# A quantised layer's head two tiles ahead, its tail reordered, and routing steps spread over shared chunks

## The reference

```python
x = x + _L0_xattn_ref(_layernorm(x, axis=-1), itok_BxS_13_99985, ctx_2048, ctx_2048, ctx_2048)
x = x + _L0_ffn_ref(_layernorm(x, axis=-1), L0_ffn_norm_w, L0_ffn_w_gv, L0_ffn_w_out)
x = x + _L1_xattn_ref(_layernorm(x, axis=-1), ctx_2048, L1_xattn_Wq, L1_xattn_Wg, L1_xattn_bg, L1_xattn_Wkv, L1_xattn_Wo)
x = x + _L1_ffn_ref(_layernorm(x, axis=-1), L1_ffn_gate_w, L1_ffn_w_gate, ..., L1_ffn_sw_down)
```

## Time and profile before

| | |
|---|---|
| median of 3 runs | 1104.53 us (1104.44 to 1106.37) |
| profiled execution | 1107.26 us |
| its span in the trace | 1105.5 us |
| busy: PE, DVE, ACT, POOL | 1048.1, 673.4, 591.9, 281.9 us |
| mean granted clock of PE | 0.986 |
| quantised layer, about | 268 to 473 us |
| attention loop, about | 485 to 665 us |
| shared part beside routing, about | 655 to 850 us |

### The profile page before, as it was taken

How to read it: one execution, slowest core, us unless ns; L and a number is a source line. 1 busy time by engine, 2 the same in 40 slices (tenths; PEclk the granted TensorE clock), 3 DMA queues, 4 the chain that set the end, 5 groups by cost and what they waited for, 6 DMA issues and landing times.

```text
span 1105.5 us, 16228 instructions
## 1 busy us (share of the span) xinstructions
PE 1048.1 (95%) x5830; PEld 824.7 (75%) x5830; DVE 673.4 (61%) x1226; ACT 591.9 (54%) x890; POOL 281.9 (26%) x445
## 2 busy tenths in 40 slices
PE   7999999979999999989999999899899999999994
PEld 5887777766455555568888888688687899999993
DVE  6746555435998998665655655466823666666660
ACT  5765787734898898853333244121113466666651
POOL 1012222113555553100000034100010044444442
PEclk9999999989999999999999999999999999999998
DMA  6682666521100000201111232302043588888853
GB/s 213 227 303 97 172 173 188 163 68 59 30 20 20 30 20 11 97 1 68 48 58 51 101 108 77 100 29 77 1 152 111 181 236 223 225 227 230 231 132 39
DMA packets 47606, 127.03 MB, mean 115 GB/s; under 512 B 5810, under 2 KB 6834, under 8 KB 46772
## 3 DMA queue, kind: packets, MB, share of 16 engines
q1 hardware_dynamic: 36516, 97.53, 26.1%
q0 software_dynamic: 10448, 27.58, 11.0%
q10 hardware_dynamic: 576, 1.05, 0.3%
HBM read 97.76 MB, written 28.38 MB: 114 GB/s over the span
## 4 chain that ended last, share of the span: by engine, by line
PE 67%; DVE 5%; ACT 3%; issue 2%; POOL 1%; DMA 0%; ACTq 0%; DVEq 0%; POOLq 0%
PE bank L54 16%; PE bank L55 15%; PE bank L56 15%; PE bank L1819 9%; PE bank L1840 4%; PE bank L3812 1%; PE bank L1831 1%; DVE s_hot_tile L3975 1%; PE bank L1913 1%; PE bank L1895 1%; DVE s_pick L3972 1%; PE bank L1924 1%; PE bank L1849 1%; PE bank L1923 1%; DVE s_mid L3999 0%
## 5 line engine op out<-in xcount | busy, mean ns | idle before, releaser
L1819 PE MATMUL bank<-w,f_qT 128*128 128x512 bf16 x512 | 117.9, 379 | 0.2 <-DVE f_h L2060 0.2
L3651 POOL DMA_INDIRECT out<-e_y,scatter_idx x32 | 69.0, 2157 | 115.7 <-ACT e_y L3746 111.5
L1819 PEld LDWEIGHTS bank<-w,f_qT 128*128 128x128 bf16 x512 | 48.7, 98 | 50.8 <-issue 0.6
L3688 ACT ACTIVATE s_m_h<-s_mid 128x512 fp32r<-128x512 f32 (+1 forms) x24 | 15.1, 631 | 126.9 <-DVE s_mid L3999 76.3
L3639 POOL DMA_INDIRECT e_xg<-xn_rows,gather_idx x32 | 33.7, 1054 | 172.6 <-DVE gather_idx L3989 105.7
L54 PE MATMUL bank<-wkv_h,ctx_h_all 128*128 128x512 f32 x128 | 54.0, 422 | 12.0 <-DVE wkv_l L708 7.4
L1840 PE MATMUL bank<-w,f_q2T 128*128 128x512 bf16 x256 | 59.5, 387 | 2.4 <-ACT f_q2T L1593 2.4
L54 PE MATMUL bank<-e_xT_h,e_wg_h 128*128 128x256 f32 (+1 forms) x192 | 56.5, 294 | 2.9 <-issue 2.1
L2060 DVE SCALAR_TENSOR_TENSOR f_h<-bank,f_columns,f_sg 128x512 f32<-128x512 f32 x64 | 47.9, 749 | 13.8 <-ACT f_sg L1577 6.8
L4077 DVE TENSOR_TENSOR e_mid<-bank,e_sil 128x256 f32<-128x256 f32 (+1 forms) x48 | 20.3, 423 | 55.5 <-ACT e_sil L3720 55.4
L55 PE MATMUL bank<-e_xT_l,e_wu_h 128*128 128x256 f32 (+1 forms) x192 | 54.1, 282 | 0.0
(11 more groups left out here) (415 smaller groups left out, 3289.9 us busy)
## 6 DMA issues: line engine op xcount, KB each, us to landing
wraw<-in_wffn SPq DMA_DIRECT2D x48, 512.0 KB, 4.2
e_raw_g<-in_ew_gate SPq DMA_DIRECT2D x16, 704.0 KB, 4.0
e_raw_u<-in_ew_up SPq DMA_DIRECT2D x16, 704.0 KB, 5.4
e_raw_d<-in_ew_down SPq DMA_DIRECT2D x16, 512.0 KB, 6.5
sorted_y<-e_y SPq DMA_DIRECT2D x19, 256.0 KB, 4.3
x_rows<-rows SPq DMA_DIRECT2D x16, 256.0 KB, 2.0
xn_rows<-a_work SPq DMA_DIRECT2D x16, 256.0 KB, 2.0
s_raw<-x_rows SPq DMA_DIRECT2D x16, 256.0 KB, 2.7
```

The lines of the kernel that those rows point to most:

```text
L1819: ins = pe.matmul(bank[c % 2][:, :], qT[t % 2][:, k * P:(k + 1) * P], w_gv(k, col + c * 512), start=(k == 0), stop=(k == KD - 1))
L3651: gp.indirect_dma_start(io["out"], bass.IndirectOffsetOnAxis(g.scatter_idx[:, slot:slot + 1], 0), e_y[t][u][:, :], None, compute_op=ALU.ad ...
L3688: ins = act.activation(m[0][r, c, :], mid[n % 2][r, :], ACT.Copy)
```

## The change

Only orders change: no instruction is added, removed or resized (PE, DVE, ACT, POOL and SP have as many as before), and functions that nothing called are deleted, which moves all line numbers. Four things are moved.

Head, on POOL, ACT and DVE:

```diff
-                for t in range(2):
+                for t in range(3):
                     scales(t)
                     largest(t)
                     steps(t)
...
-                    if have(i + 2):
+                    if i and have(i + 2):
                         scales(i + 2)
                         largest(i + 2)
...
                 residual(0)
+                quantise(1)
                 context(3)
...
-                context(2)
                 round_q(0)
                 invert(1)
+                context(2)
+                statistics(2)
+                weigh(2)
                 context(3)
+                round_q(1)
+                invert(2)
                 summary()
```

Tail and attention, on ACT, PE and DVE:

```diff
                 high(TT - 1)
-                normalise(TT - 2)
-                phi(0)
                 copy_q2T(TT - 1, 0)
                 copy_q2T(TT - 1, 1)
-                split_q(0)
+                normalise(TT - 2)
+                query(0)
...
                 bias()
+                query(2)
                 normalise(TT - 1)
-                query(2)
+                query(3)
                 split_x(TT - 1)
-                query(3)
...
                 query(1)
+                contract(TT - 1)
                 turn_x(TT - 2)
-                contract(TT - 1)
                 query(2)
                 query(3)
+                gate(0)
                 turn_x(TT - 1)
-                gate(0)
+                query(4)
                 for s in range(TT):
                     if s:
                         turn_att(s - 1)
                     attend(s)
-                    if s + KD < TT:
-                        query(s + KD)
+                    if s + KD + 1 < TT:
+                        query(s + KD + 1)
                     if s:
                         project(s - 1)
...
                 query(2)
+                query(3)
                 split_x(TT - 1)
-                query(3)
```

Shared part and routing, on ACT, PE and DVE:

```diff
                 shared["softmax"]()
+                shared["split_w"](12)
                 shared["activate"](3)
-                shared["split_w"](12)
                 shared["split_w"](13)
-                shared["activate"](4)
                 shared["split_w"](14)
                 act.wait_ge(x3_late, 16 * (TT - EARLY))
+                shared["activate"](4)
                 shared["split_w"](15)
+                shared["split_w"](16)
                 shared["activate"](5)
-                shared["split_w"](16)
...
                 last.then_inc(o_ready, 1)
+                if b == 0 and t == 1:
+                    count()
...
-                if b == 0:
-                    count()
+                if b == 1:
+                    place(0)
                 contract(b)
+                if b == 1:
+                    place(1)
                 if b + 1 < B:
                     for c in range(1, SFT):
                         expand(b + 1, c)
-                        if b == 1 and c >= 2:
-                            place(c - 2)
+                        if b == 1 and c in (2, 4):
+                            place(c // 2 + 1)
...
+            product_low(3)
+            ties()
+            product_low(4)
+            product_low(5)
+            masks()
+            product_rows_low(6, ([(weights,)], [(orders,)], [(totals,)], []))
+            product_low(7)
+            places()
+            product_low(8)
+            picks()
+            product_low(9)
+            chosen(row, krow)
+            chosen(tile, ktile)
+            product_low(10)
+            chosen(wn, kw)
+            split_parts()
+            product_low(11)
+            hot_rows(0)
+            hot_parts(0)
+            product_rows_low(12, ([(hot_rows, 1)], [(hot_parts, 1)], [], []))
+            hot_rows(2)
+            hot_parts(2)
+            product_low(13)
+            product_low(14)
+            hot_rows(3)
+            hot_parts(3)
```

More of the change, by code:

```diff
@@ L1250, in there @@
-def there(t, pairs):
-    return not isinstance(t[0], int) or 0 <= t[0] < pairs
 def ffn0_to_experts1(nc, g, io):
@@ L1685, in _ @@
                         copy_q2T(i - 2, 1)
-                    if have(i + 1):
+                    if i and have(i + 1):
                         quantise(i + 1)
@@ L3966, in split_parts, with hot_rows @@
             then(v.tensor_copy(kparts[:, 4, :], rest[:, 2, :]))
-        def hot(q):
+        def hot_rows(q):
             lo, hi = q * PART, (q + 1) * PART
@@ L4012, in product_low, with product_rows_low @@
             product(n)
-            if n % SFT == 0 and n:
-                for t in range(4):
-                    residual(4 * (n // SFT - 1) + t)
+            low(n)
+        def product_rows_low(n, between):
+            product(n)
+            for t, step in enumerate(between):
+                residual(4 * (n // SFT - 1) + t)
+                for do, *which in step:
+                    do(*which)
             low(n)
@@ L4021, in shared @@
             best()
-            for n in range(seam_chunks, LAST):
-                product_low(n)
-                if n == seam_chunks:
-                    ties()
-                if n == seam_chunks + 1:
-                    masks()
-                if n == seam_chunks + 2:
-                    weights()
-                if n == seam_chunks + 3:
-                    orders()
-                if n == 7:
-                    totals()
-                if n == 8:
-                    places()
-                if n == 9:
-                    picks()
-                if n == 10:
-                    chosen(row, krow)
-                    chosen(tile, ktile)
-                if n == 11:
-                    chosen(wn, kw)
-                    split_parts()
-                if 12 <= n < 16:
-                    hot(n - 12)
-                if n == 17:
-                    find()
+            product_low(3)
[24 more added lines that the diff above has]
+            hot_parts(3)
+            product_low(15)
+            product_low(16)
+            find()
+            product_low(17)
+            product_rows_low(18, ([], [], [], []))
+            for n in range(19, LAST):
+                product_low(n)
         def e_split_w(e, part):
```

1434 lines of the change are left out of this document (2 added, 1432 removed).

## The result

The changed kernel takes **1154.6 us** (median of four runs, 1151.5 to 1157.8) where the kernel before takes 1105.5 in the same session: ratio **1.043**, 95% interval 1.041 to 1.046. The forecast was 1140 us with a range of 1128 to 1150: the direction was right, the time lies 4.6 us outside the range. The profiled execution spans 1151.6 us, 46.1 more than before.

A forecast was written before the change was run, and what follows sets the result against it. TensorE's own order was taken as the bound. Head -1.4, tail, first query and its clock -1.5 + 2.3, loop +29.0 + 8.5, routing -1.5 gave +35.4 us on 1104.53: 1140 us, range 1128 to 1150.

The forecast's parts named there:

- the loop's mechanism: Attention loop: query(s + 5) waits for phi(s + 4), which DVE does behind a_weigh(s); ten waits of 2.9 us, +29.0 us.
- The clock: Slow TensorE stretches behind the loop's waits: half of ten at 1.7 us, +8.5 us, plus 2.3 us behind query(5)'s wait.
- The upper bound of +17: Attention loop: upper bound of the clock term for the ten waits of 2.9 us; the lower bound was 0.
- every one of the ten waits drops the clock: Rival for the attention loop: all ten waits are followed by the low clock, +8.5 us more, 1148 us; chance 0.13.
- Tail and first query: Quantised layer's tail -3.8, attend(0)'s wait filled by query(4) -2.7, turn_x(15) +0.6; query(5)'s wait of +4.4 counted separately makes -1.5.
- Head: Head of the quantised layer: earlier rounding lets the first product end PE's wait sooner, -1.4 us, bounds 0 and -4.1.
- Routing: Routing steps: weight-split wait gone -5.0, one-hot waits gone -7.0, new wait before place(0) +8.2, its clock +2.3; sum -1.5 us.
- The other side: Rival for the attention loop: phi(s + 4) is done before attend(s) ends, so no wait, 1096 us; chance 0.04.

The follow-up runs named there:

- phi_first: Changed kernel with phi(s + 4) moved ahead of split_att(s - 1) and a_weigh(s) on VectorE and ScalarE, TensorE's order kept: 1111.4 us, 1.0033.
- phi_ahead: Changed kernel with feature maps moved along with the queries on VectorE and ScalarE, phi(4) ahead of the loop, phi(s + 5) in turn s: 1099.5 us, 0.9927.
- head_only: Kernel before with the head's change alone (steps of tiles 1 and 2 ahead of the last context tiles and the summary): ratio 0.9995.
- tail_only: Kernel before with the tail's change alone (q2 copies earlier, contract(15) behind query(1), turn_x(15) behind gate(0)), attention loop as before: ratio 0.9984.
- loop_back: Changed kernel with the attention loop's query order put back (query(s + 4) behind attend(s), none ahead of the loop): 1102.1 us, 0.9955.
- half_gate: Changed kernel with half of gate(s + 1), six products of 128x512, between attend(s) and query(s + 5): 1115.4 us, 1.008.
- routing_only: Kernel before with the routing steps' change alone (ScalarE's order, count() in contract(0), placements and one-hot matrices spread): ratio 0.9999.
- gate_pad: Changed kernel with the whole gate(s + 1) between attend(s) and query(s + 5), plus five idle VectorE sums ahead of phi: 1179.4 us, 1.065.

## Why the prediction was right and where it was wrong

**What bounds it, and the loop's mechanism: right.** PE's order sets the end, and `query(s + 5)` made it wait for a `phi` that stands behind `a_weigh`. Forecast 2.9 us ten times and 4.4 once, 33.4 in all; measured 2.73 and 4.1, 31.5. phi_first and phi_ahead show that the place of `phi` was the cause.

**The clock: wrong, and this is the step that failed.** "For the ten waits of 2.9 us I take half, +8.5 us", and 2.3 for the first, 10.8 in all. Measured 24.0. Both factors were low: ten of eleven waits fell, not six, and each cost 2.4 us, not 1.7. With 24.0 in place of 10.8 the sum is 1153 us. I had pooled six waits of the kernel before, in one execution, as if they were draws of one kind and as if the loop's would be more of it. All eleven of the loop stand behind twelve narrow products; none of the six did. That this made the odds worse is likely, as said above, and not shown; the six don't sort themselves by it, for the 3.8 us wait fell behind twelve products of 128x512. And "2.69 us passed" was one execution's luck: the same wait fell in head_only, tail_only and loop_back. The upper bound of +17 was ten times 1.7; the loss of a slow stretch had a higher row, the 3.0 us behind the stage's start, and the bound should have used it. The rival "every one of the ten waits drops the clock", kept at 0.13, was nearer to what this loop did, though at 1.7 us each it too stops at 1148 us, and as a rule it fails on half_gate's eleven waits. Why ten of eleven fell, and at 2.4 us each, stays open.

**Tail and first query, -5.9: right in size** (-6.4: 3.6 by the tail, 2.8 by the query that fills the wait), and in part by luck. The 3.8 us for the tail held 1.7 us for the slow contraction. In routing_only, with the old order, the contraction ran at 1.00, a wait ahead of `turn_x(15)` was longer, and `attend(0)` still came 27.55 us behind `query(0)`, as against 27.53. So the 1.7 us did not count there, and the 3.6 came from `a_q_first` being ready earlier. The filled wait ahead of `attend(0)` also took away a place for the low clock to follow, which it did in three of the four traces that have the wait.

**Head, -1.4: right in the traces** (-1.2; the first wait for `f_q` gone, one of 0.8 for `f_h` in its place, the second of 1.9 still there). In the time it can't be told from nothing.

**Routing, -1.5: right as a sum** (-1.3 between the first two traces, -1.6 between the means above) and in its largest part (`place(0)`: 8.2 forecast, 8.5 measured). The wait for the down-projection's weights is gone, with a new one of 1.7 us for `s_mid` ahead of it that I had not seen: its 0.7 before grew by 1.0.

**The rivals.** The other side (1096) failed as its condition did: the wait was 2.7 us, not under 0.8. Its price was near: 8.8 us gained, where phi_ahead, which removes the waits, takes 1099.5, 6.5 less than the kernel before in its session.

**The remaining 2.6 us** in the profile come from stages that the diff doesn't touch; the summary starts between 246.6 and 252.0 us in the seventeen traces.

## What to carry to other kernels

When an engine's work is moved one step further ahead, look at what its buffer's reader does in that same turn: a lead on one engine is worth nothing, and costs a stall in every turn, unless the readers take the same lead (1154.6 us without, 1099.5 with). Price a stall of PE of 2 us or more, in a loop, at itself plus the slow stretch behind it as the upper bound, and take that stretch from the longest such row. Waits of 1.3 to 1.6 us behind wide products cost only themselves here; one of 0.7 us behind narrow products did not always. A row that shows one wait passing at full clock is one draw: ask for a second execution before it carries a term.

## What the runs showed of the hardware that I had not expected

The clock's answer to equal waits is a matter of odds: 2.85 us passed and 2.86 us didn't, in one execution, 15 us apart. Waits of 2.0 us behind narrow products were enough in eight cases of ten, and one of 0.73 us in four of 25. And the loss behind one wait isn't fixed: 1.4 to 1.7 us (clock 0.70 to 0.74 over 5.6 us) in some cases, 2.4 to 2.8 (0.50 to 0.58) in others, once 2.1 (0.62, in gate_pad); the changed kernel's last six slow stretches, at a period of 17 us, were all of the second kind.
